# Layer 0 of a two-layer image block: step sizes and decays made in token layout, recurrent states held in PSUM

## What is computed

```python
x_norm = layernorm(x) ; xz = x_norm @ in_proj_W          # 256 -> 2 * 384
x_proj, z = xz[..., :384], xz[..., 384:]
windows = 2x2 windows of x_proj                          # 4 tokens each
def light_s6(x, xproj_W, dt_W, dt_b, A_log, D):          # once forwards, once on flipped tokens
    proj = x @ xproj_W                                   # 48 for dt, 8 for b, 8 for c
    dt = silu(proj[..., :48] @ dt_W + dt_b)              # [window, token, 384]
    dA = exp(dt[..., None] * -exp(A_log))                # 8 states
    state = dA_t * state + dt * b_t * x_t                # over the 4 tokens, state0 = 0
    y_t = sum over states of state * c_t
    return y + x * D
y_conv = gelu(depthwise3x3(x_proj) @ pw_W)
y = (alpha * 0.5 * (y_fwd + y_bwd) + (1 - alpha) * y_conv) * silu(z) @ out_W
x_out = x + y
return x_out + gelu(layernorm2(x_out) @ fuse_W1 + b1) @ fuse_W2 + b2
```

## Time and profile before

| | |
|---|---|
| median of 3 runs | 5837.58 us |
| the profiled execution, span from first to last instruction | 5842.9 us |
| that execution's place | 5.3 us over the median, inside the runs' 5837.41 to 5845.89; only its span is known, no time around it |
| busy: TensorE (PE) | 5433.9 us, 93% |
| busy: VectorE (DVE) | 4398.7 us, 75% |
| busy: ScalarE (ACT) | 3394.4 us, 58% |
| busy: GpSimd (POOL) | 584.8 us, 10% |
| DMA, mean over the span | 34 GB/s |

### The profile page before, as it was taken

One profiled execution on the slowest core, in us unless ns is written; L12 is line 12 of the kernel. 1 busy time (PEld: TensorE's weight loads), 2 busy tenths in 40 slices (PEclk: granted clock), 3 DMA queues, 4 the chain that ended last, 5 costly groups with the idle time before them and its releaser, 6 DMA issues. The chain is left out here.

```text
span 5842.9 us, 100627 instructions
## 1 busy us (share of the span) xinstructions
PE 5433.9 (93%) x30696; PEld 4376.2 (75%) x30696; DVE 4398.7 (75%) x8598; ACT 3394.4 (58%) x5910; POOL 584.8 (10%) x658
## 2 busy tenths in 40 slices
PE   5999999999999999999999998899999999999998
PEld 4666666667667666666666665699889989988998
DVE  4888888887888788788878886676666667766666
ACT  3666666666666666666666664355555555555554
POOL 0111111111111110111111110100000000000000
PEclk8999999999999999999999999899999999999999
DMA  1010010010010010010000000300300030012000
GB/s 41 13 36 28 26 37 25 28 37 23 30 37 23 27 40 23 27 34 30 27 29 34 27 24 33 108 19 19 96 29 19 19 98 19 24 46 73 19 19 18
DMA packets 140892, 198.71 MB, mean 34 GB/s; under 512 B 19760, under 2 KB 107920, under 8 KB 140272
## 3 DMA queue, kind: packets, MB, share of 16 engines
q1 hardware_dynamic: 140272, 190.95, 10.3%
HBM read 111.22 MB, written 79.69 MB: 33 GB/s over the span
## 5 line engine op out<-in xcount | busy, mean ns | idle before, releaser
L1335 ACT ACTIVATE probs<-ps_s 128x512 f32<-128x512 f32 x1024 | 612.3, 598 | 1037.6 <-PE ps_s L1288 1037.6
L1346 DVE TENSOR_REDUCE part_max<-ps_m 128x1 f32<-128x512 f32 x1056 | 717.2, 691 | 576.1 <-PE ps_m L1268 575.9
L1297 PE MATMUL ps_o<-vh,ph 128*128 128x258 f32 x4096 | 1045.7, 288 | 31.6 <-ACT ph L1337 31.6
L1298 PE MATMUL ps_o<-vl,ph 128*128 128x256 f32 x4096 | 1037.1, 285 | 0.0
L369 PEld LDWEIGHTS psD<-ident,dec 128*128 128x128 f32 x4608 | 572.5, 144 | 491.0 <-DVE p_st L868 142.3
L369 PE MATMUL psD<-ident,dec 128*128 128x128 f32 x4608 | 784.2, 284 | 160.0 <-ACT dec L653 79.3
L868 DVE TENSOR_TENSOR p_st<-s_st,psD 128x384 f32<-128x384 f32 x1024 | 561.8, 549 | 490.0 <-PE psD L369 486.0
L419 PE MATMUL psF<-xp,conv_w 128*128 128x256 f32 x3456 | 862.4, 398 | 10.7 <-ACT u L608 10.3
L1297 PEld LDWEIGHTS ps_o<-vh,ph 128*128 128x128 f32 x4096 | 789.4, 193 | 48.1 <-issue 23.5
L653 ACT ACTIVATE dec<-dt,decay 128x384 f32<-128x384 f32 x1536 | 804.6, 603 | 2.3
L1298 PEld LDWEIGHTS ps_o<-vl,ph 128*128 128x128 f32 x4096 | 789.5, 193 | 0.0
(11 more groups left out here) (145 smaller groups left out, 7055.8 us busy)
## 6 DMA issues: line engine op xcount, KB each, us to landing
values_d<-v_st SPq DMA_DIRECT2D x64, 512.0 KB, 4.8
xf<-in_x_dram SPq DMA_DIRECT2D x128, 128.0 KB
xb<-in_x_dram SPq DMA_DIRECT2D x128, 128.0 KB
residual_d<-xb SPq DMA_DIRECT2D x32, 512.0 KB, 2.6
vh<-values_d SPq DMA_DIRECT2D x32, 512.0 KB, 5.0
vl<-values_d SPq DMA_DIRECT2D x32, 512.0 KB, 6.0
res<-residual_d SPq DMA_DIRECT2D x32, 512.0 KB, 3.3
out_dram<-res SPq DMA_DIRECT2D x128, 128.0 KB
```

The lines of the kernel that those rows point to most:

```text
L1297: pe.matmul(ps_o[qt][:, 0:C + 2], lhs, vh[:, m, :], start=m == 0, stop=False, skip_group_check=True)
L1298: pe.matmul(ps_o[qt][:, 0:C], lhs, vl[:, m, :], start=False, stop=False, skip_group_check=True)
L1335: nc.scalar.activation(probs[:, m % 3, :], ps_s[m % 2][:, :], ACT.Exp).then_inc(exp_ok, 1)
L1346: nc.vector.tensor_reduce(part_max[:, qt, kc:kc + 1], ps_m[r % 2][:, :], AX.X, ALU.max).then_inc(max_out, 1)
```

## The change

- `dt` in token layout: for each token one product with `proj_sb` as the stationary side, 128x384, and a second product of two rows that adds the bias (`two`, `dtb_row`); `Silu` without a bias (L601). 8 of them a tile, where 6 of 128x512 were. The backward ones move from ticks 0 to 2 to ticks 5 to 8.
- `x` in token layout: `inx` is also copied to `x_ch` (the memory of `y_ch`), turned (`xk0` to `xk2`) and copied to `x_win`. GpSimd makes `u = dt * x_win` (`umf`, `umb`), so the turning and copying of `ut` goes.
- Rates: `exp(A_log)` is loaded over all partitions, `rates[128, 2, 8, 384]`. GpSimd multiplies `dt` by it, 3 products of 128x384 per state and direction (48 a tile, `exponents`), into `dec`, a ring of 4. ScalarE exponentiates with scale -1: the first decay straight into the state's PSUM bank (`psS`, 3 banks), the other two in place in `dec` in one instruction of 768 columns. 16 such pairs a tile at the ticks of `EXP_AT`. All turning of decays goes.
- States in PSUM: p, s work in place on the bank. The last of the 16 chains has its state in `dec` (SBUF). Chains are no longer in pairs: 3 ticks a chain (a slot), the first half of chain q alternating with the second half of chain q-1.
- `w10` to `w12` of BACK and `proj`, `bct`, `gd`, `inx` of NEXT are at other ticks.
- Memory: `h2` and `v_st` lie in `hid`, `fg_raw` in `gel`, which adds waits (`v_stored` before the second layernorm's output, `r_ok` before `fg0`, `fg_ok` before `pw0`). One decay table, two bias columns and their loads go from `prepare`.

```diff
 OWN = {
-    0: ["dtb0"], 1: ["dtb1"], 2: ["dtb2"], 5: ["z0"], 6: ["z1"], 8: ["z2", "conv0a"], 10: ["conv0b"],
+    5: ["dtb0"], 6: ["z0", "dtb1"], 7: ["z1", "dtb2"], 8: ["z2", "dtb3", "conv0a"], 10: ["conv0b"],
...
-DECAYS_AT = [3, 9, 14, 20, 26, 32, 39, 43]
+EXP_AT = {1: 1, 4: 2, 5: 3, 9: 4, 12: 5, 16: 6, 18: 7, 21: 8, 24: 9, 26: 10, 31: 11, 33: 12, 38: 13, 40: 14, 43: 15}
+EXP_FIRST = 46
+RING = 4
...
+FIRST_HALF = ["p1", "s1", "y1", "p2"]
+SECOND_HALF = ["s2", "y2", "p3", "y3"]
...
+        def state(q):
+            return psS[q % STATE_BANKS][:, 0:INNER] if q < CHAINS - 1 else dec[:, q % RING, 0, :]
...
+                    pe.matmul(bank[:, 0:INNER], proj_sb[r0:r0 + RANK, t * P:(t + 1) * P],
+                              dt_w[r0:r0 + RANK, :], start=True, stop=False)
+                    mm = pe.matmul(bank[:, 0:INNER], two[:, :], dtb_row[:, d, :], start=False, stop=True)
...
+            def decays(k, q):
+                act.wait_ge(arg_ok, CHAINS * k + q + 1)
+                if q < CHAINS - 1 and not (exact(k) and k == 0 and q < STATE_BANKS):
+                    act.wait_ge(state_ok, chain_done(k, q - STATE_BANKS if q >= STATE_BANKS else q - STATE_BANKS - 1, "y3"))
+                nc.scalar.activation(state(q), dec[:, q % RING, 0, :], ACT.Exp, scale=-1.0).then_inc(exp_ok, 1)
+                nc.scalar.activation(dec[:, q % RING, 1:, :], dec[:, q % RING, 1:, :], ACT.Exp,
+                                     scale=-1.0).then_inc(exp_ok, 1)
...
+            def exponents(k, q):
+                d, n = q // STATES, q % STATES
+                pool.wait_ge(front_out, front_job(k, f"dt{'fb'[d]}3"))
+                if not (exact(k) and k == 0 and q < RING):
+                    pool.wait_ge(state_ok, chain_done(k, q - RING, "p3" if q != RING - 1 else "y3"))
+                for j in range(1, T):
+                    last = nc.gpsimd.tensor_tensor(dec[:, q % RING, j - 1, :], dt[:, d, token_of(d, j), :],
+                                                   rates[:, d, n, :], ALU.mult)
+                last.then_inc(arg_ok, 1)
...
+                    if tick % SLOT == 0:
+                        q = tick // SLOT + 2
```

More of the change, by code:

```diff
@@ L508, in back @@
                 mm.then_inc(back_full, 1)
[L510 to L527, removed]
             def body(k, par, part):
                 for tick, todo in ticks(k, part):
-                    if part not in ("front", "back"):
-                        turn_decays(k, par, tick // 6, tick % 6)
                     for step, tile, where in todo:
@@ L562, in front @@
                         act.wait_ge(halo_ok, f + 1)
-                        if not (exact(f) and f == 0):
-                            act.wait_ge(u_mul, 6 * f)
+                    nc.scalar.activation(x_ch[:, cb, dr * 256:(dr + 1) * 256], bank[:, 0:TOK // 2], ACT.Identity,
+                                         bias=in_bias[:, cb:cb + 1])
                     dst = xp[:, cb, 1 + dr:dr + ROWS:2, 1:W + 1].rearrange("p wr (wc dc) -> p dc wr wc", dc=2)
@@ L581, in front @@
                 elif job.startswith("dt"):
-                    d, cb = "fb".index(job[2]), int(job[3])
-                    if not (exact(f) and f == 0):
-                        act.wait_ge(u_mul, 6 * (f - 1) + 3 * (d + 1))
-                    last = nc.scalar.activation(dt[:, d, cb, :], bank[:, :], ACT.Silu,
-                                                bias=col[:, dtb_c[d][cb]:dtb_c[d][cb] + 1])
+                    d, t = "fb".index(job[2]), int(job[3])
+                    if t == 0 and not (exact(f) and f == 0):
+                        act.wait_ge(u_mul, multiplied(f - 1, d, T - 1))
+                        act.wait_ge(arg_ok, CHAINS * (f - 1) + STATES * (d + 1))
+                    last = nc.scalar.activation(dt[:, d, t, :], bank[:, 0:INNER], ACT.Silu)
                 elif job.startswith("z"):
@@ L631, in back @@
                         act.wait_ge(fg_stored, 96 * g)
+                    act.wait_ge(r_ok, CB * TILES if exact(g) and g == TILES - 1 else CB * (g + 2))
                     nc.scalar.activation(fg_raw[0:2 * CK, :], bank[0:2 * CK, :], ACT.Identity,
@@ L658, in body @@
             def body(k, par, part):
                 for tick, todo in ticks(k, part):
-                    if tick in DECAYS_AT and part != "back":
-                        slot = DECAYS_AT.index(tick)
-                        if slot == 2 * PAIRS - 1 if part == "front" else part != "tail" or slot < 2 * PAIRS - 1:
-                            decays(k, slot + 1)
+                    if exact(k) and k == -1 and tick == 30:
+                        turn_rates()
+                    if tick in EXP_AT and part not in ("front", "back"):
+                        decays(k, EXP_AT[tick])
@@ L666, in body @@
+                    if tick == EXP_FIRST and part not in ("tail", "back"):
+                        decays(k + 1, 0)
                     for step, tile, where in todo:
@@ L705, in body @@
                             last.then_inc(bias2_ok, 1)
+                    if tick % SLOT == 0:
+                        q = tick // SLOT + 2
+                        if q < CHAINS and part not in ("front", "back"):
+                            exponents(k, q)
+                        elif q >= CHAINS and part not in ("tail", "back"):
+                            exponents(k + 1, q - CHAINS)
+            pool.wait_ge(rates_ok, 2)
             iterations(pool, body)
@@ L730, in norm_step @@
                     dve.wait_ge(ok, base + 4)
+                    if out is h2 and not (exact(tile) and tile == 0):
+                        dve.wait_ge(v_stored, 32 * tile)
                     for i in range(n):
@@ L872, in states @@
                                                        ALU.mult, ALU.add).then_inc(state_ok, 1)
                     else:
[L874 to L881 removed]
+                        y_t = y_tok[:, par, t, :]
```

293 lines of the change are left out of this document (145 added, 148 removed), and 13 rows, old and new, of tables (BACK, NEXT, OWN).

## The result

The changed kernel takes 6334.77 us, median of four runs (6327.99 to 6337.62), against 5837.49 us for the kernel before in the same session (5831.98 to 5845.89). The ratio is 1.0843, 95% interval 1.0827 to 1.0858 (the quotient of the two medians, 1.0852, lies inside it): 8.4% slower. The forecast had the sign, 6050 us and an upper end of 6200; it is 285 us short.

A forecast was written before the change was run, and what follows sets the result against it. TensorE bounded the tile before (102 us busy); the new tile, walked along its waits, took 114.9 us against 108.4, so 6.5 x 31 = +202, plus 8 at the start: 5843 + 210 = 6053, given as 6050 us. Range 5740 to 6200.

The forecast's parts named there:

- step 3: TensorE from `z1` to the second `out` half: 4.7 us of gate and step-size jobs, then 10.8; ends 27.3 after E.
- Steps 1, 2, 4 to 7 and 9: Pieces on VectorE, ScalarE and GpSimd, ending 8.8, 11.8, 42.6, 48.7, 51.0, 55.1 and 78.8 us after E.
- steps 2, 5 and 8: ScalarE's chain 3 exponentials ahead of step sizes (11.8), GpSimd's adds ahead of chain 8 (48.7), TensorE's `proj` to `inx` (73.7).
- the walk: Waits followed from E, VectorE's end of a tile's last chain, to the next E: 114.9 us against 108.4.
- step 8: TensorE's `proj`, four `w1`, three `pw`, `bct` and two `inx`, ending 73.7 us after E.
- step 10: TensorE's `inx4`, `w20`, `inx5`, `xk1`, `dtf0`, `w21`: 10.2 us, ending 89.0 after E.
- The second rival: TensorE's clock halves at tile starts, so the first 4.7 us of jobs cost 4.7 more: 6200 us, chance 0.12.
- Step 11: VectorE's add, slots 12 to 14 and last slot of 10.2 us, ending the tile 112.7 us after E.
- Step 12: Loop's back edge: 4.33 us every second tile, 2.2 a tile, bringing the tile to 114.9.
- The start: Before the first chain, loading and exponentiating the rates adds 8 us, bounds 0 and 20.
- the third rival: GpSimd's products cost 1.4 us each, lengthening the tile by 2.2 us: 6120 us, chance 0.10.
- the first: Rival: the couplings don't bite and VectorE's own work sets a 96 us period: 5467 us, chance 0.28.

The follow-up runs named there:

- e9: Combined kernel plus two fillers of products nobody reads, 11 ahead of each E and 9 between `dtb1` and `yt2`: 6046.01 us.
- e13: Changed kernel, order untouched, plus five products nobody reads in TensorE's wait ahead of `proj`: 6258.48 us.
- combined kernel: Changed kernel with chain 3's exponentials late, `w10` and `w11` ahead of `proj`, bias adds behind chain 8's arguments, and rates early: 5966.61 us.
- e2: Changed kernel with ScalarE's exponentials of chain 3 moved behind the backward step sizes and gates: 6171.42 us.
- e6: Changed kernel with ScalarE's two exponentials of the rates moved ahead of tile 0's first layernorm: 6325.09 us.
- e1: Changed kernel plus 11 products nobody reads at the end of each tile on TensorE: 6329.02 us.
- e4: Changed kernel with four tiles in the loop's body in place of two: 6300.80 us.

## Why the forecast was short

Of the 285 us, 261 lie in the periods (14.9 us longer for 6.5, 31 times) and 23 ahead of them. Step by step for the tile from E = 1604.90, us after E (it follows a loop edge; in the tiles that don't, each point from step 3 on is 0.6 to 0.9 later):

| point | forecast | measured |
|---|---|---|
| 1: y3 of chain 0 | 8.8 | 8.5 |
| 2: first dt Silu done | 11.8 | 11.6 |
| 3: second `out` done | 27.3 | 29.9 |
| 4: norms done | 42.6 | 44.9 |
| 5: arguments of chain 8 | 48.7 | 50.7 |
| 6: `xnt0` evacuated | 51.0 | 53.0 |
| 7: `xnth` split | 55.1 | 57.2 |
| 8: second `inx` | 73.7 | 78.2 |
| 9: bank of inx2 free | 78.8 | 83.5 |
| 10: `w21` done | 89.0 | 95.9 |
| 11: next E, no edge | 112.7 | 122.2 |

- **Steps 1, 2, 4 to 7 and 9 were right**, each within 0.5 us of its own length. That steps 2, 5 and 8 bind was argued before and is now shown, one run each.
- **Steps 3, 8 and 10 were priced at full clock, and this is what failed first.** They took 2.8, 2.4 and 2.2 us more than forecast, 7.4 of the 11.4 us that an inner tile is longer than walked. Some 5.6 of it is the clock: `proj` and `w10` 5.9 us for 3.2; `inx4` and `w20` 1.3 over their rows; `z1` to `dtb3` 7.2, where e9 has 5.6 at a granted 1.00. Some 1.3 are prices: a step-size product with its bias costs 1.2 us at full clock, where the walk had 0.85 as an estimate, three times in steps 3 and 10, and the rest is the gate products. e13 shows the clock of step 8 to be on the path and to give back 2.5 us. For step 3 it wasn't isolated: with full clock there, e9 gained 1.6 us in a tile of the combined kernel. For step 10, e2 had the clock up and the rows short, beside its own change. The second rival had the mechanism, with a chance of 0.12, one place and 4.7 us there, where the rows have 1.6; its condition, TensorE standing, came true at every long wait that the walk itself had put there. The Trainium skill, "TensorE: Matmul & The Clock Gate", section "Part 1: The HAM clock gate", says that idle stretches halve the clock. By that rule the jobs behind a wait in a walk carry a surcharge. The trace agrees at the three places in the changed kernel; but e2 has a wait of 2.85 us ahead of `inx4` with the clock at 1.00 behind it, so such a wait doesn't always cost.
- **Step 11 was 26.3 us for 23.7.** 1.8 is a wait on ScalarE for chain 13 that the walk didn't have (the exponentials stand behind step sizes in ScalarE's list; 5.5 us once `w2` came early). 1.4 is in the last slot, 11.6 for 10.2, where `fg_lo` takes 1.45 us and chain 15's steps in SBUF up to 1.34. Slots 12 to 14 were 0.5 shorter than forecast.
- **Step 12**: the edge's stall is 7.4 us, not 4.33 as in the earlier trace rows; 3.7 a tile for 2.2. That it would stay was assumed, not read.
- **The base of the sum**: 114.9 is the walk of a tile inside layer 0, and the 108.4 it was held against is a mean with the last two distances, 99.0 and 51.3 us, in it. Inside, the kernel before has 110.9. The slip made the forecast 2.5 us a tile longer, so it hid part of the error: inside, the tile is 11.4 us longer than walked.
- **The start**: forecast 8, measured 31. The rates cost 12.7 where they stand, of which e6 took back 9.3 (their columns at 1.9 ns, not the 1.35 that the rows of shorter ones gave), the later start of the first layernorm 1.4 (the bias row is prepared ahead of it), and 17 is the slower pace of the first two tiles, which is the period's and not a start's.
- **Prices** of GpSimd (1047 ns mean for 1.0 us), of ScalarE (0.49 + 0.83 for 1.3) and of a write to PSUM (nothing: 613 ns for 0.61) held; the third rival is out. So is the first, for this order: its 5467 needs every coupling gone, and with most of them gone the kernel stands at 5806.

## What to carry over

When a change gives the bounding engine less to do but puts waits into its list, price the jobs behind each long wait at that engine's lower clock too, from a row that has it, and put it into the forecast and not only into a rival. When an operation moves to another engine, ask of every fixed list it enters what now stands behind it: two such places were worth 163 and 88 us, and a third, where products had left a wait empty, 98. Each is an edit of one line, and the three simply added up. And hold a walk of an inner tile against the distance of inner tiles.

## What was unexpected of the hardware

- Behind a pause of 3.4 us ahead of `yt0` the clock was 0.50, though TensorE had been filled for 7 us before (e1, e9). In e13 pauses of 1.3 and 0.7 us left it at 1.00. Behind a pause of 2.9 us ahead of `inx4` it was down in the changed kernel and up in e2.
- In the changed kernel the clock stayed at 0.50 through 9 us of work without a gap, from 1597.0 on.
- Useless products made the kernel 1.2% faster in e13 and 1.3% slower than the combined one in e9. In e13 they ended right at the job that they were for; in e1 and e9 the first filler ended 3.3 to 3.5 us ahead of it.
- VectorE works in place on a PSUM bank at the price of SBUF: 613 and 618 ns, where the kernel before has 0.61 us.
- The stall at the loop's edge isn't a constant: 2.8 to 4.4 us before, with two tiles in the body as with four (to 4.5); 6.6 to 7.6 in the changed kernel, 8.5 to 9.3 with four tiles (e4). What sets it, the runs don't show.
